# The second feed-forward product of a transformer-like block as seven half-size products (Strassen's scheme), with the residual parked in memory

## The reference, cut to what matters

```python
def ternarize(W, threshold):
    absW = jnp.abs(W); delta = threshold * jnp.max(absW)
    mask = absW > delta
    n = jnp.maximum(jnp.sum(mask), 1)
    alpha = jnp.sum(jnp.where(mask, absW, 0.0)) / n
    return alpha * jnp.sign(W) * mask
h = x3n @ ternarize(W1).T + b1     # x3n: layer norm of x; h: 1024 x 4096
h = gelu(h)
y = h @ ternarize(W2).T + b2       # 1024 x 1024
scale = max(|y|) / 7 + 1e-8        # over the whole tensor
out = x + clip(round(y / scale), -7, 7) * scale
```

## Time and profile before

| | |
|---|---|
| median of 3 runs | 1466.53 us (1466.33 to 1467.66) |
| profiled execution, its own time | 1467.44 us |
| its span, first to last instruction | 1465.6 us |
| mean granted TensorE clock | 0.987 |
| stage A, first to last matmul | 1002.7 to 1224.9 us |
| stage B, first to last matmul | 1225.1 to 1445.9 us |
| busy over the span | PE 96%, DVE 48%, ACT 25% |

### The profile page before, as it was taken

How to read it: one execution, slowest core, us unless ns; L and a number is a source line. 1 busy time by engine, 2 the same in 40 slices (tenths; PEclk the granted TensorE clock), 3 DMA queues, 4 the chain that set the end, 5 groups by cost and what they waited for, 6 DMA issues and landing times.

```text
span 1465.6 us, 16778 instructions
## 1 busy us (share of the span) xinstructions
PE 1410.4 (96%) x6834; PEld 673.7 (46%) x6834; DVE 706.7 (48%) x1204; ACT 373.0 (25%) x590; POOL 2.4 (0%) x10
## 2 busy tenths in 40 slices
PE   6979999999999799999999999999999999999994
PEld 4534445435445244445555555444444444444442
DVE  3223423424324488837777775845887831003006
ACT  1111202202112122124443432014666652000003
POOL 0000000000000000000000000000000000000000
PEclk9999999999999899999999999999999999999997
DMA  9999999999988776743434332320766631111112
GB/s 381 420 421 417 421 421 412 412 389 405 402 318 325 287 241 247 280 140 126 136 124 148 118 101 94 130 72 29 194 186 188 187 87 54 40 36 40 38 31 114
DMA packets 103771, 315.52 MB, mean 215 GB/s; under 512 B 39824, under 2 KB 48400, under 8 KB 82192
## 3 DMA queue, kind: packets, MB, share of 16 engines
q1 hardware_dynamic: 101680, 307.12, 56.9%
q10 hardware_dynamic: 2016, 7.34, 1.2%
HBM read 289.79 MB, written 24.64 MB: 215 GB/s over the span
## 4 chain that ended last, share of the span: by engine, by line
PE 78%; issue 16%; DMA 4%; DVE 2%; ACT 0%; SPq 0%; DVEq 0%; POOLq 0%; POOL 0%; ACTq 0%
PE ps L836 15%; PE ps L960 15%; PE ps L766 11%; PE ps L822 8%; PE ps L912 8%; PE ps L676 7%; PE ps L718 4%; PE ps L697 4%; DMA ctx_sb<-in_ctx 4%; PE ps L748 2%; PE ps L858 1%; PE ps L700 1%; PE ps L876 1%; PE ps L813 1%; PE ps L659 0%
## 5 line engine op out<-in xcount | busy, mean ns | idle before, releaser
L836 PE MATMUL ps<-x2T,wqk_sb 128*128 128x512 f32 x512 | 224.1, 594 | 0.0
L973 PE MATMUL ps<-t_half,h_hi 128*128 128x512 f16 x512 | 194.0, 379 | 0.0
L973 PE MATMUL ps<-t_half,h_lo 128*128 128x512 f16 x512 | 194.0, 379 | 0.0
L766 PE MATMUL ps<-ctx_sb,attnT 128*64 128x512 f32 (+1 forms) x832 | 180.5, 593 | 1.7 <-DMA ctx_sb<-in_ctx 1.7
L836 PEld LDWEIGHTS ps<-x2T,wqk_sb 128*128 128x128 f32 x512 | 95.6, 190 | 112.9 <-issue 112.4
L500 ACT ACTIVATE stg<-ps 128x512 f32<-128x512 f32 (+1 forms) x80 | 44.3, 554 | 357.4 <-PE ps L697 310.5
L960 PE MATMUL ps<-x3h,t_buf 128*128 128x512 f16 x512 | 121.0, 379 | 0.0
L960 PE MATMUL ps<-x3l,t_buf 128*128 128x512 f16 x512 | 120.9, 379 | 0.0
L676 PE MATMUL ps<-ctxT,x1T 128*64 128x512 f32 x512 | 116.6, 601 | 0.0
L766 PEld LDWEIGHTS ps<-ctx_sb,attnT 128*64 128x64 f32 (+1 forms) x832 | 59.2, 137 | 117.1 <-issue 109.9
L822 PE MATMUL ps<-wv_sb,x2T 128*128 128x512 f32 x256 | 112.0, 596 | 0.0
(11 more groups left out here) (164 smaller groups left out, 1397.2 us busy)
## 6 DMA issues: line engine op xcount, KB each, us to landing
ctxT<-in_ctxT SPq DMA_DIRECT2D x64, 1024.0 KB, 15.5
ctx_sb<-in_ctx SPq DMA_DIRECT2D x16, 4096.0 KB, 20.5
ctx_sb<-in_ctx SPq DMA_DIRECT2D x16, 2048.0 KB, 11.2
w_scan<-in_w1t SPq DMA_DIRECT2D x32, 512.0 KB, 5.1
w_buf<-in_w1t SPq DMA_DIRECT2D x32, 512.0 KB, 3.8
w_scan<-in_w2t SPq DMA_DIRECT2D x32, 512.0 KB, 4.6
t_dram<-t_out SPq DMA_DIRECT2D x64, 256.0 KB, 2.1
w_buf<-in_w2t SPq DMA_DIRECT2D x32, 512.0 KB, 3.9
```

The costliest lines, as they stand in the source:

```text
L766: ins = mm(bank(ea + hf)[C * b:C * b + C, :], attnT[0:w, slots[mt], C * b:C * b + C], ctx_sb[0:w, mt, b, hf * BANK:hf * BANK + BANK], star ...
L836: ins = mm(bank(b0 + hf), wqk_sb[:, w, c, :], x2T[:, c, hf * BANK:hf * BANK + BANK], start=(c == 0), stop=(c == NC - 1))
L973: ins = mm(bank(t), part[:, t * P:t * P + P], t_half[:, hc % 8, :], start=(hc == 0 and n == 0), stop=(hc == HC - 1 and n == 1))
```

## The change

**The scheme.** The second product is split into 2 x 2 blocks: two token halves of 512 by two hidden halves of 2048 (HK = 16 chunks), and two hidden halves by two output halves of 512. The form with seven products is used in which running sums are shared. Product m has a left factor (a block of h, or a sum of blocks) and a right factor (a block of ternary weights B11, B12, B21, B22, or one of four sums T1 to T4, small integers that f16 holds exactly). `LEFT` and `RIGHT` name them. Each product has 16 steps (`k`), each step 4 token tiles (`s`) x 2 parts (`n`). A step is numbered r = 16 m + k, from 0 to 111. Products 2, 4 and 6 go on adding in the banks of the product two before (`fresh` is false).

**Left factors.** h is now kept as fp32 in `hq` (128 KB of each partition); Gelu and scaling write it in place. For each step ACT copies `hq` to f16 (`high`) and DVE subtracts to get the low part (`lower`) into a ring `hl` of RING = 12 steps. Before products 1, 2, 4 and 5 DVE forms sums in place in `hq` (`sum_1` to `sum_4`, 16 of 128 x 512 each).

**Right factors.** `ternary2` after every second tile also makes T1 to T4 (4 operations of 128 x 512, f16), and SP stores a set of 8 blocks (1 MB). `t_half` is a ring of BRING = 8 pieces of 128 KB, one for a step. The first 8 are loaded behind stage A, each later one when the step 8 before is done.

**The residual.** It is written to DRAM (`put_away`) before stage A and fetched back as `xo2` (two transfers of 2 MB), after the last sum and ahead of the load for step 96. `b2` is loaded earlier.

**Results.** Each finished product is taken out by `collect` (28 in all, 16 of them with a maximum). The last LAST_K = 8 steps run with the token tile outside.

The core of the diff:

```diff
-            for q in range(2):
-                for hc in range(HC - 4):
-                    if q == 0 and hc == 4:
-                        pe.wait_ge(h_ready, 2 * HC)
-                    pe.wait_ge(t2_in[hc % 8], 16 * (HC // 8 * q + hc // 8 + 1))
-                    for t in range(NT):
-                        ins = product(q, hc, t)
-                    ins.then_inc(t2_used, 1)
...
+            def operands(r):
+                pe.wait_ge(b_in[r % BRING], 16 * (r // BRING + 1))
+                pe.wait_ge(lo_ready, r + 1)
+
+            for n in range(7 * HK - LAST_K):
+                operands(n)
+                for s in range(4):
+                    ins = product(n, s)
+                if n % HK < HK - 1:
+                    ins.then_inc(k_used, 1)
+            for n in range(7 * HK - LAST_K, 7 * HK):
+                operands(n)
+            for s in range(4):
+                for n in range(7 * HK - LAST_K, 7 * HK):
+                    product(n, s)
...
+        def consumed(eng, r):
+            if r % HK == HK - 1:
+                eng.wait_ge(y_done, 4 * (r // HK) + 4)
+            else:
+                eng.wait_ge(k_used, r + 1 - r // HK)
...
+            for n in range(BRING):
+                load_B(n)
+            for n in range(BRING, 7 * HK):
+                if n == 6 * HK:
+                    sp.wait_ge(s_ready, 4 * HK)
+                    for i in range(2):
+                        sp.dma_start(xo2[:, 4 * i:4 * i + 4, :], x_dram[:, 4 * i:4 * i + 4, :]).then_inc(x_back, 16)
+                consumed(sp, n - BRING)
+                load_B(n)
...
+            def high(r):
+                m, k = r // HK, r % HK
+                if r >= RING:
+                    consumed(act, r - RING)
+                if m in SUMS:
+                    act.wait_ge(s_ready, HK * SUMS[m] + k + 1)
+                A(hl[:, r % RING, 0, :], hq[:, LEFT[m], k, :], ACT.Copy).then_inc(hi_ready, 1)
...
+                if n % 2:
+                    B11, B12, B21, B22, T1, T2, T3, T4 = (t2_set[:, k % 2, i, :] for i in range(8))
+                    own.done(V.tensor_tensor(T3, B22, B12, ALU.subtract))
+                    own.done(V.tensor_tensor(T2, T3, B11, ALU.add))
+                    V.tensor_tensor(T1, B12, B11, ALU.subtract).then_inc(t2_full, 1)
+                    V.tensor_tensor(T4, B21, T2, ALU.subtract).then_inc(t2_full, 1)
...
+            sums = {2: sum_2, 4: sum_3, 5: sum_4}
+            for r in range(RING, 7 * HK + 2):
+                if r // HK in sums:
+                    sums[r // HK](r % HK)
+                if r >= RING + 2:
+                    n = r - 2
+                    lower(n)
+                    if n % HK == RING - 1 and n >= HK:
+                        for s in range(4):
+                            collect(n // HK - 1, s)
+            for s in range(4):
+                collect(6, s)
...
+            V.wait_ge(x_back, 32)
```

More of the change, by code:

```diff
@@ L63 @@
 HC = HID // P
-LO0 = 26
 WT = HID * N // P // 1024
@@ L70 @@
 X_SCALE = 1024.0
-H_RANGE = 32000.0
+H_RANGE = 8000.0
 ROUND = 1.5 * 2.0 ** 23
@@ L141, in build @@
         wqk_sb = sb("wqk_sb", [P, 2, NC, P], 192 * KB)
-        w_scan2 = sb("w_scan2", [P, 4, 1024], 184 * KB)
+        w_scan2 = sb("w_scan2", [P, 4, 1024], 84 * KB)
         x3s = [sb("x3s0", [P, N], 48 * KB), sb("x3s1", [P, N], 116 * KB)]
[L144 to L151, removed]
+        x3h = sb("x3h", [P, NC, NT * P], 160 * KB, F16)
+        x3l = sb("x3l", [P, NC, NT * P], 176 * KB, F16)
+        w2_buf = sb("w2_buf", [P, 2, 1024], 0)
+        t2_set = sb("t2_set", [P, 2, 8, BANK], 8 * KB, F16)
+        hl = sb("hl", [P, RING, 2, BANK], 0, F16)
+        t_half = sb("t_half", [P, BRING, BANK], 24 * KB, F16)
+        hq = sb("hq", [P, 4, HK, BANK], 32 * KB)
+        xo2 = sb("xo2", [P, NT, N], 96 * KB)
+        y = sb("y", [P, NT, N], 160 * KB)
         t_buf = sb("t_buf", [P, 4, 1024], 192 * KB, F16)
-        t_half = sb("t_half", [P, 8, BANK], 192 * KB, F16)
-        g_buf = sb("g_buf", [P, 2, BANK], 200 * KB)
         b2_bc = sb("b2_bc", [P, N], 200 * KB)
-        y = sb("y", [P, NT, N], 84 * KB)
         at = [204 * KB]
@@ L432, in _ @@
             for i in range(2):
[L433 to L446, removed]
+                sp.wait_ge(t2_stored[i], 16 * (HK // 2))
+            sp.wait_ge(x_out[3], 16)
+            for n in range(BRING):
[7 more added lines that the diff above has]
+                load_B(n)
             for t in range(NT):
@@ L627, in _ @@
                     act.wait_ge(t2_ready, n + 1)
-                    A(w2_buf[:, n % 2, :], t2_out[:, n % 2, :], ACT.Square, accum_out=wacc[:, 1, n:n + 1])\
-                        .then_inc(t2_counted, 1)
+                    A(w2_buf[:, n % 2, :], t2_set[:, n // 2 % 2, 2 * (n % 2):2 * (n % 2) + 2, :].rearrange("p a n -> p (a n)"), ACT.Square,
+                      accum_out=wacc[:, 1, n:n + 1]).then_inc(t2_counted, 1)
+                if m == 2 * HC - RING:
+                    for i in range(2):
+                        act.wait_ge(t2_stored[i], 16 * (HK // 2))
+                    act.wait_ge(t2_counted, WT)
+                if m >= 2 * HC - RING:
+                    high(m - 2 * HC + RING)
+            act.wait_ge(h_out, 2 * HC)
+            for n in range(RING, 7 * HK):
+                high(n)
             act.wait_ge(d_vec, 2)
@@ L962, in _, with product @@
                 ins.then_inc(h_done, 1)
-            def product(q, hc, t):
-                for n in range(2):
[L967 to L975, removed]
+            def product(r, s):
+                m, k = r // HK, r % HK
+                b = 4 * (m % 2) + s
+                if k == 0:
+                    if m < 2:
+                        pe.wait_ge(g_ready, 2 * HC - 7 + b)
+                    else:
+                        pe.wait_ge(y_out, 4 * (m - 2) + s + 1)
+                fresh = m in (0, 1, 3, 5)
+                for n in range(2):
+                    ins = mm(bank(b), hl[:, r % RING, n, s * P:s * P + P], t_half[:, r % BRING, :],
+                             start=(fresh and k == 0 and n == 0), stop=(k == HK - 1 and n == 1),
+                             skip_group_check=not fresh)
+                if k == HK - 1:
@@ L1302, in _, with left, sum_1, sum_2 @@
             low_part(NT - 1)
[L1305 to L1317, removed]
+            def left(m, k):
+                return hq[:, LEFT[m], k, :]
+            def sum_1(k):
+                V.wait_ge(h_out, H_ORDER.index((HK + k, 1)) + 1)
+                V.tensor_tensor(left(1, k), left(1, k), hq[:, 3, k, :], ALU.add).then_inc(s_ready, 1)
+            def sum_2(k):
+                V.wait_ge(lo_ready, HK + k + 1)
+                V.tensor_tensor(left(2, k), left(2, k), hq[:, 0, k, :], ALU.subtract).then_inc(s_ready, 1)
+            def sum_3(k):
+                V.wait_ge(s_ready, HK + k + 1)
+                V.tensor_tensor(left(4, k), hq[:, 3, k, :], hq[:, 2, k, :], ALU.subtract).then_inc(s_ready, 1)
+            def sum_4(k):
+                V.wait_ge(lo_ready, 3 * HK + k + 1)
+                V.tensor_tensor(left(5, k), left(5, k), hq[:, 2, k, :], ALU.subtract).then_inc(s_ready, 1)
+            def lower(r):
+                V.wait_ge(hi_ready, r + 1)
+                V.tensor_tensor(hl[:, r % RING, 1, :], left(r // HK, r % HK), hl[:, r % RING, 0, :], ALU.subtract)\
+                    .then_inc(lo_ready, 1)
+            threshold(1)
+            for m in range(2 * HC):
+                if H_ORDER[m] in T2_AFTER:
+                    ternary2(T2_AFTER[H_ORDER[m]])
+                if m >= 1 and H_ORDER[m - 1][1] == 1 and H_ORDER[m - 1][0] >= HK:
+                    sum_1(H_ORDER[m - 1][0] - HK)
+                if m > 2 * HC - RING:
+                    lower(m - 1 - 2 * HC + RING)
+            sum_1(HK - 1)
+            lower(RING - 1)
             totals(1, t2_ready, t2_counted)
@@ L1323, in _, with collect @@
             V.wait_ge(b2_in, 16)
[L1324 to L1332, removed]
+            at_y = lambda row, col, s: y[:, 4 * row + s, BANK * col:BANK * col + BANK]
+            bias = lambda col: b2_bc[:, BANK * col:BANK * col + BANK]
+            found = [0]
+            def collect(m, s):
+                V.wait_ge(y_done, 4 * m + s + 1)
+                if m >= 2:
+                    V.wait_ge(y_out, 4 * (m - 2) + s + 1)
+                to, more = {0: (at_y(0, 0, s), bias(0)), 1: (at_y(1, 1, s), bias(1)),
+                            2: (at_y(0, 1, s), at_y(1, 1, s)), 3: (at_y(0, 0, s), at_y(0, 0, s)),
+                            4: (at_y(1, 1, s), at_y(1, 1, s)), 5: (at_y(0, 1, s), at_y(0, 1, s)),
+                            6: (at_y(1, 0, s), bias(0))}[m]
+                V.scalar_tensor_tensor(to, bank(4 * (m % 2) + s), yscale[:, 0:1], more, ALU.mult, ALU.add).then_inc(y_out, 1)
+                if m >= 3:
+                    V.wait_ge(y_out, 4 * m + s + 1)
+                    i = found[0]
```

(5 more changed lines are left out.)

75 lines of the change are left out of this document (47 added, 28 removed).

## The result

| | before | changed |
|---|---|---|
| median | 1466.43 us (1465.92 to 1467.66, 4 runs) | 1444.01 us (1441.94 to 1444.83, 4 runs) |
| span of the profiled execution | 1465.6 us | 1440.1 us |
| its own time | 1467.44 us | 1441.94 us |

The ratio is 0.9844, 95% interval 0.9827 to 0.9861: faster by 22.4 us, inside the forecast range of 1438.5 to 1446. Note that the profiled execution is the shortest of the four. The others took 1443.51, 1444.5 and 1444.83 us. Where these 2 us come from is the question of the experiments.

A forecast was written before the change was run, and what follows sets the result against it. PE was taken as the bound, stage B costing its matmuls times 0.2158 us. -27.6 for removed matmuls and +2.5 for the gap, others 0, gave -25.1: 1442.3, adjusted towards the median to 1441.4 us; range 1438.5 to 1446.

The forecast's parts named there:

- -27.6 us: Stage B: 1024 matmuls become 896, and each of the 128 removed is worth its full spacing of 0.2158 us.
- Stage A at 0: Stage A stays PE-bound despite the new DVE, ACT and queue work; cost 0.
- cover of over 10 us: Stage A: slack claimed for each added work; first weights needed about 20 us after the loads and stores ahead.
- no other wait of PE behind 1007 us: Sign of being right: behind 1007 us PE waits only before step 104, for 2.2 to 3.3 us.
- The rings at 0: Stage B: weight pieces and left factors come in time, with 12 us and 19 us of lead; cost 0.
- The gap before step 104: Last block: PE waits for step 111's weight piece, issued only when step 103 is done; +2.5 us, bounds 2.2 to 3.3.
- The way back at 0: Piece 96, queued behind the residual's 4 MB, lands after 12.3 us, due after 13.8 us: no stall, cost 0.
- estimate of 11.9 us: Way back: time for the 4 MB by the skill's fit of 2.0 us plus bytes over 436 GB/s; no stall.
- rival of the way back: The residual's 4 MB stall step 96 too: +2.0 us, 1443.4 us; chance 0.10.
- first rival: Clock falls to half for 3.4 us at the gap before step 104, losing 1.7 us: 1443.1 us; chance 0.28.

The follow-up runs named there:

- experiment 8: Last block of 4 steps, and every matmul of product 0 issued twice (128 matmuls put back), against the kernel before: 1467.27 us, ratio 1.0002.
- experiment 7: Ring of left factors cut from 12 steps to 4, on the kernel with a last block of 4 steps: 1449.19 us.
- experiments 2: Changed kernel with a last block of 4 steps instead of 8 (LAST_K = 4), rings unchanged: 1439.49 us.
- experiment 3: Changed kernel with a last block of 7 steps instead of 8 (LAST_K = 7): 1439.64 us.
- experiment 6: Changed kernel with the load for step 111 made twice, the second only when the first has landed: 1446.68 us.
- experiment 4: Changed kernel with the residual's 4 MB issued ahead of the load for step 111 instead of step 96: 1452.84 us.
- experiment 5: Changed kernel with every product, not only the last, ending in a block of 8 steps: 1463.73 us.

## Why the prediction was right

**The bound and the matmuls.** The spacing stayed 0.2158 us under DVE at 68% and with two waits in each step, and experiment 8 shows that -27.6 us is the whole of the gain, to within its interval.

**Stage A at 0.** The last matmul of stage A and the first of stage B follow as before. The price of an f16 sum was 0.42 us, near the lower of the two bounds (0.37 and 0.69). The cost was nearly 0, but not by the cover of over 10 us that the prediction gives. The loads of the first weights behind SP's 1 MB stores landed later (median 6.7 us for 4.4 before), and the first of them had no 20 us: issued at 1024.5 us, it landed at 1031.2, and its chunk was due then:

```profile
1031.28 1.41 PEld L1003 LDWEIGHTS ps<-x3h,t_buf 128*128 128x128 f16 x8 [0.40 <-DMA t_buf<-t_dram]
```

The matmuls behind it came 0.1 us late here and up to 0.2 late in the other traces of this kernel (0.4 in experiment 7). The kernel before had 1.5 us to spare at this place (1025.8 to 1030.3). So the prediction's "no other wait of PE behind 1007 us" was not quite met; that the slip was this small is luck.

**The rings at 0.** Right, with a sum and a subtraction every 1.2 us in the densest part, as these lines of the order of time in product 5's sums show:

```profile
1345.10 0.69 DVE L1378 TENSOR_TENSOR hq<-hq 128x512 f32<-128x512 f32 x1
1345.70 0.69 DVE L1382 TENSOR_TENSOR hl<-hq,hl 128x512 f16<-128x512 f32 x1
1346.30 0.68 DVE L1378 TENSOR_TENSOR hq<-hq 128x512 f32<-128x512 f32 x1
```

**The gap before step 104.** Forecast 2.5 us, measured 2.47 (the idle time is 2.31, and 2.25 to 2.36 in the others), in its place and for its cause (experiments 2 and 3).

**The way back at 0.** Right in the traces of the changed kernel, but with 0.6 us of cover, and 0.3 in one of them, where the sum gave 1.5: the piece landed 12.7 us after the 4 MB were issued (forecast 12.3), and was due 13.3 us after it instead of 13.8, because SP came to it half a microsecond after step 87 had ended. In the trace of experiment 6 the cover did not hold and PE lost 0.4 us, so the rival of the way back happens too, in small. Experiment 4 shows the queue order that the sum only assumed. The Trainium skill, "DMA: Bandwidth & Descriptors", section "Queues, rings and completion order", has this order; the trace agrees, with 11.3 us for a piece that else takes 2.0. The prediction's estimate of 11.9 us takes its fit from a section on transfers that GpSimd issues; SP issued these, and the piece took 12.7.

**The clock.** Forecast and first rival differed in one chance event, and both happened: ten executions of fifteen lie near the forecast (1441.4 us; measured 1441.07 to 1442.82), five near the rival (1443.1; measured 1443.45 to 1444.83). That ten to five looks like the chances given, 0.45 to 0.28, is luck, since the share went from three of four to none of seven between repeats. The price of one fall in a trace was right, 1.7 us against 1.55 to 1.57 (experiment 5). The median of the first four lies 2.6 us above the forecast. Drawing three of the upper group makes 1.8 of that; the median of all fifteen is still 0.8 above, which is no more than the kernel before moved between sessions (medians 1466.16 to 1467.25).

What stays open: no trace of the upper group of the changed kernel itself was caught. That its loss is this fall is argued from the mean clock (0.985, which the execution of experiment 6 with one fall also has, for 0.987), from the same gap with and without a fall in experiment 5, and from block 4, where gap and upper group are both missing. Against it: the groups lie 2.3 us apart and one fall costs 1.6, so 0.7 us is not accounted for, and the one run at 0.984 asks for more than one such fall. A longer fall (2.0 us in experiment 4) or a late piece 96 (0.4 us in experiment 6) could supply the rest; neither was tested.

The Trainium skill, "TensorE: Matmul & The Clock Gate", section "HAM oscillation — how this bites in real kernels", describes a falling clock for waits that come back in every turn of a loop: the clock falls in each and the matmuls behind it start at half rate. Experiment 5 has that pattern and agrees in kind, but only in part: of the six gaps of 2.3 to 2.8 us two were followed by a fall, four were not.

## What to carry to other kernels

When PE is saturated, a removed matmul is worth its spacing (here 0.2158 us), and new work on the other engines costs next to nothing as long as each ring's lead in time exceeds the latency of its refill plus the longest block of other work on the engine that refills it. Check that lead at the start of a stage too, where it can be shorter than in its middle. Compare each ring's length with every place where the consumer waits for several slots at once: a block as long as the ring exposes a whole refill, a transfer (2.3 us idle) or a copy and a subtraction (1.5), and one step less is almost a cure (0.6). A large transfer in the queue of small ones delays them by its full length, so it needs its place chosen by the due time of the next small one, and that place moves when an engine upstream gets slower.

## What the runs showed that was not expected

An idle PE of 2.3 us between dense matmuls can be followed by some 3.4 us at half clock, which costs 1.6 us beyond the gap. In the traces this came after two of eleven gaps of 2.2 to 2.8 us: two of the six of experiment 5, none of the five of the changed kernel. After each of the three longer ones (3.97, 4.40 and 11.55 us) it came, and after the 0.57 us of experiment 3 it did not. So few cases give no rate. That the same fall makes the two groups of times of the changed kernel is likely, and not shown.
